# Earlier first transposes, a split up product and moved value copies in a macaron attention block

## The chip, the cores and the metric

The kernel runs on one core of a Trainium2 chip. The metric is the device time of one execution in microseconds (us). Of the kernel before there are three timed runs: 263.29, 265.15 and 265.61, median 265.15 us. One more execution was profiled.

## What is computed

One block of the "macaron" form on x of 2048 rows by 128 features, all in float32. `ffn` is a feed-forward network whose inner part is two butterfly transforms of nine stages; attention is over 16 heads of 8 features and is sparse: a query sees every fourth key, and all keys up to 8 positions away.

```
x = x + 0.5 * ffn(layernorm(x))
x = x + attn(layernorm(x))
x = x + 0.5 * ffn(layernorm(x))

ffn(x):   h = x @ W_exp + b_exp                       # 128 -> 512
          h = gelu(butterfly(h, up_weights) + up_bias)
          y = butterfly(h, down_weights) @ W_con + b_con + down_bias

attn(x):  q, k, v = x @ q_w, x @ k_w, x @ v_w ; q *= sigmoid(unity_scale)
          allowed = (j % 4 == 0) | (abs(i - j) <= 8)
          softmax(where(allowed, q @ k.T / sqrt(8), -inf)) @ v @ o_w + o_b
```

## The kernel before, in words

**Shape of the work.** The 2048 rows are four blocks (`NB`) of 512, each of four tiles (`TB`) of 128 rows. Since nothing non-linear stands inside a butterfly, each is folded with its dense matrix into one 128x512 (`UPW`) or 512x128 (`DNW`) weight while the kernel starts. The order of each engine is written out by hand, an engine runs its own list in order, and semaphores join the lists. PSUM, the memory TensorE writes, has eight banks of 512 columns, `PS[:, 0..7]`.

**The prologue.** TensorE spreads the far stages' weights over all partitions (`spread`), runs a filler product (`keep_warm(1, 1)`, whose output nobody reads), multiplies the folded stages with W_exp (`upw_ps`), transposes the first normalized block (`transpose_block(0)`), makes the bias (`bup_ps`), runs two more fillers (`keep_warm(6, 2)`) and then the first up product (`ffn_up(0)`). VectorE does the stages of folding. ScalarE first takes the sigmoid's exponential of one number that a DMA brings (`ld_un`), then loads the Gelu table, normalizes the first block, copies the spread weights (`SEVENS`), makes eight scaled copies of W_con (`CON8`) and only then copies the transposed block to `XT` (`operand(0)`).

**The first FFN and the projections.** For each block: up product, Gelu on ScalarE, down product (`ffn_down`), sum and layernorm on VectorE, transposes (`turn_rows`), and keys, queries and values (`keys_queries`, `block_values`). VectorE splits keys and queries into three bf16 parts, and SyncE writes the parts to DRAM and loads them back in the layout of attention: the strided keys by `write_strided` and `load_strided`, the local ones by `write_local` and `load_k`. TensorE may start on the strided scores of block c of the keys only when `ld_ks[c]` has come. A test decides whether the softmax needs its maxima: `bound_product` on VectorE makes a number per partition, `count_kept` on TensorE counts them, `bound_flag` on VectorE sets the flag. In the fourth down product the count stands at its half.

**Attention.** 4 blocks by 4 groups of heads give 16 units of nine steps: eight steps of strided scores (two heads by one block of keys, 128x1024 results) and one of local scores. ScalarE takes the exponential of each, VectorE masks the local one (`mask_local`), TensorE forms the value products (`values`, `values_local`), and VectorE and TensorE turn and scale the result (`turn`, `finish_unit`). The last block's own values are computed inside unit 0, after its third step: `block_values(NB - 1)` writes one strided tile and five local ones to banks 6 and 7, and ScalarE's `values_out(NB - 1)` copies them to `VS` and `VL`. Units write their results alternately in banks 6 and 7, so unit 1 may use bank 7 only when it has been copied out.

**The second FFN.** After the last unit: `values(3)`, `values_local`, which waits for VectorE's mask, `transpose_block(NB)`, `turn`, `ffn_up(NB)`, `ctx_turn` and `project`, then three more blocks.

## Time and profile before

| quantity | value |
|---|---|
| median of three runs (lowest to highest) | 265.15 us (263.29 to 265.61) |
| the profiled execution, whole | 265.68 us |
| its span in the trace | 263.7 us |
| TensorE busy | 248.0 us, 94% |
| ScalarE busy | 191.1 us, 72% |
| VectorE busy | 125.4 us, 48% |
| share of TensorE in the chain that ended last | 90% |
| an exponential of 128x1024 on ScalarE | 1.02 us |
| a table load on ScalarE | 1.28 us |
| a whole down product of 32 matmul records | 3.74 us |
| end of VectorE's last split of keys and queries | at 80.3 us |
| start of the fourth step of unit 1 on TensorE | at 84.6 us |

The profile shows when each engine worked on what, by line of the kernel; idle time is given with the event that ended it. A float32 product is recorded as two matmuls and two weight loads, so "x8" is four products. Weight loads of TensorE (PEld) run beside its matmuls (PE). SPq and ACTq are the DMA instructions that SyncE and ScalarE issue.

### The profile page before, as it was taken

Reading aid. Unit: us, or ns where it says so; the run is one execution under the profiler, and the core shown is the slowest. Engines: PE = TensorE matmul, PEld = TensorE weight load, DVE = VectorE, ACT = ScalarE, POOL = GpSimd, SP = SyncE. Lnnn points to the kernel's source line nnn. Section 1 sums busy time; section 2 is a strip of 40 time slices with the busy share of each in tenths; the row PEclk is TensorE's granted clock in tenths of the full one; section 3 lists DMA queues with packets and bytes.
Section 4 is the critical chain, followed back from the end, with each engine's and each line's share of the span. In section 5 each row is a group of like instructions: output and inputs, shape, how many; then the busy total and the mean of one; then the engine's idle time right before and its main releaser. Section 6 shows DMA issues by size and latency. Waiting matters only on the chain.

```text
span 263.7 us, 6909 instructions
## 1 busy us (share of the span) xinstructions
PE 248.0 (94%) x2914; PEld 138.3 (52%) x2914; DVE 125.4 (48%) x408; ACT 191.1 (72%) x245; POOL 7.4 (3%) x12
## 2 busy tenths in 40 slices
PE   0998899998889999999999999999999999899995
PEld 0466585857444444445434455444454444457775
DVE  3689949687793133226234225314325521546013
ACT  1735337383789999988999988999978999653440
POOL 0910000000000000000000000000000000000000
PEclk9999999999999999999999999999999999999999
DMA  5840000386689660330331231232030000000112
GB/s 162 238 137 14 2 0 0 114 240 175 162 208 358 220 144 27 85 88 2 87 86 25 65 87 27 62 87 71 18 87 2 0 2 4 2 0 0 42 40 80
DMA packets 23894, 21.42 MB, mean 81 GB/s; under 512 B 4619, under 2 KB 22095, under 8 KB 23843
## 3 DMA queue, kind: packets, MB, share of 16 engines
q1 hardware_dynamic: 23270, 20.88, 29.2%
q8 instruction: 23, 0.38, 0.6%
q10 hardware_dynamic: 592, 0.09, 0.2%
q14 instruction: 9, 0.07, 0.1%
HBM read 13.60 MB, written 7.56 MB: 80 GB/s over the span
## 4 chain that ended last, share of the span: by engine, by line
PE 90%; ACT 3%; DVE 2%; DMA 2%; issue 1%; ACTq 0%
PE ps L699 23%; PE ps L677 23%; PE ps L517 10%; PE ps L465 9%; PE ps L684 4%; PE ps L709 4%; PE ps L470 2%; PE ps L717 2%; DMA prologue_or_parts<-far_sel 2%; PE ps L553 2%; PE ps L729 1%; PE ps L474 1%; PE ps L448 1%; ACT v_local L841 1%; PE ps L540 1%
## 5 line engine op out<-in xcount | busy, mean ns | idle before, releaser
L902 ACT ACTIVATE probs_all<-ps 128x1024 f32<-128x1024 f32 x128 | 122.8, 1023 | 10.1 <-PE ps L677 9.7
L699 PE MATMUL ps<-probs_all,v_strided 128*32 128x256 f32 x1024 | 68.2, 384 | 1.2 <-ACT v_local L841 1.2
L677 PE MATMUL ps<-q_slots,k_strided 75*128 75x512 bf16 x256 | 66.7, 381 | 0.2 <-ACT probs_all L825 0.2
L699 PEld LDWEIGHTS ps<-probs_all,v_strided 128*32 128x32 f32 x1024 | 27.2, 109 | 32.8 <-issue 9.5
L677 PEld LDWEIGHTS ps<-q_slots,k_strided 75*128 75x128 bf16 x256 | 20.9, 97 | 34.0 <-ACT probs_all L902 9.5
L1210 DVE RECIPROCAL rden<-ps 128x16 f32<-128x16 f32 x16 | 4.1, 258 | 72.1 <-PE ps L717 72.1
L465 PE MATMUL ps<-xnorm_t,up_folded 128*128 128x512 f32 x64 | 29.2, 599 | 1.0 <-ACT xnorm_t L790 1.0
L799 ACT ACTIVATE gelu_h<-ps,bias_up 128x512 f32<-128x512 f32 x24 | 16.1, 687 | 13.0 <-PE ps L465 13.0
L517 PE MATMUL ps<-down_folded,gelu_h 128*128 128x128 f32 x192 | 23.1, 278 | 0.9 <-ACT down_folded L866 0.7
L517 PEld LDWEIGHTS ps<-down_folded,gelu_h 128*128 128x128 f32 x192 | 22.0, 192 | 2.0 <-ACT down_folded L866 0.9
L1236 DVE SCALAR_TENSOR_TENSOR probs_all<-probs_all,mask_k_sb 128x1024 f32<-128x1024 f32 x16 | 19.6, 1224 | 4.0 <-ACT probs_all L908 3.5
L908 ACT ACTIVATE probs_all<-ps 128x1024 f32<-128x1024 f32 x16 | 16.4, 1023 | 3.7 <-PE ps L684 2.1
L465 PEld LDWEIGHTS ps<-xnorm_t,up_folded 128*128 128x128 f32 x64 | 11.7, 192 | 14.0 <-issue 11.9
L1075 DVE SCALAR_TENSOR_TENSOR resid<-ps,resid 128x512 f32<-128x512 f32 (+1 forms) x10 | 5.8, 584 | 22.3 <-PE ps L517 22.3
L1207 DVE COPY o_sb<-ps 128x256 f32<-128x256 f32 x16 | 6.8, 425 | 12.4 <-PE ps L709 12.2
L684 PEld LDWEIGHTS ps<-q_slots,k_local 75*64 75x64 bf16 x512 | 9.3, 112 | 5.9 <-ACT probs_all L902 5.3
L969 DVE TENSOR_SCALAR xnorm<-resid,mean_var,rstd 128x128 f32<-128x128 f32 x44 | 12.1, 342 | 0.2
L709 PEld LDWEIGHTS ps<-probs_all,v_local 128*32 128x32 f32 x512 | 7.9, 109 | 7.8 <-issue 4.7
L935 DVE BATCH_NORM_STATS2 stats<-resid 128x6 f32<-128x128 f32 x48 | 10.3, 280 | 3.1 <-DMA resid<-L_attn_x 2.9
L709 PE MATMUL ps<-probs_all,v_local 128*32 128x64 f32 x512 | 10.5, 222 | 1.0 <-DVE probs_all L1236 1.0
L684 PE MATMUL ps<-q_slots,k_local 75*64 75x64 bf16 x512 | 11.1, 197 | 0.0
L799 ACT ACTIVATE probs_all<-ps,bias_up 128x512 f32<-128x512 f32 x8 | 5.5, 687 | 6.5 <-PE ps L465 6.5
(137 smaller groups left out, 219.2 us busy)
## 6 DMA issues: line engine op xcount, KB each, us to landing
q_slots<-q_parts SPq DMA_DIRECT2D x16, 288.0 KB
k_local<-k_local_parts SPq DMA_DIRECT2D x48, 78.0 KB
q_parts<-prologue_or_parts SPq DMA_DIRECT2D x9, 384.0 KB, 4.4
k_strided<-k_strided_parts SPq DMA_DIRECT2D x12, 96.0 KB
q_parts<-last_parts SPq DMA_DIRECT2D x3, 384.0 KB, 4.9
k_local_parts<-prologue_or_parts SPq DMA_DIRECT2D x3, 288.0 KB, 5.0
resid<-L_attn_x SPq DMA_DIRECT2D x1, 768.0 KB, 8.5
out<-resid SPq DMA_DIRECT2D x3, 256.0 KB, 2.3
```

The lines of the kernel that those rows point to most:

```text
L465: pe.matmul(PS[:, 1 + c, :], UPW[:, c * P:(c + 1) * P], XT[:, :], start=True, stop=True).then_inc(h_ps, 1)
L517: mm = pe.matmul(down_bank(b, t)[:, t * P:(t + 1) * P], hidden(b)[:, c, t * P:(t + 1) * P], DNW[:, c, :], start=(c == 0), stop=(c == NC - 1))
L677: mm = pe.matmul(PS[:, b0 + i, :], KS[:, ch, G * g + h, :], QS[:, g, h, :], start=True, stop=True)
L684: mm = pe.matmul(PS[r * W:(r + 1) * W, b0 + h // 2, (h % 2 * TB + t) * W:(h % 2 * TB + t + 1) * W], KL[:, g, h, w * WSTEP:w * WSTEP + W], ...
L699: mm = pe.matmul(PS[VC * h:VC * (h + 1), 6 + n % 2, 0:QB // 2], VS[:, ch, at:at + VC], probs, start=(ch == 0 and r == 0), stop=False, skip ...
L709: mm = pe.matmul(PS[VC * h:VC * (h + 1), 6 + n % 2, t * W:(t + 1) * W], VL[:, TB * it + t, at:at + VC], PL[:, h, t, :], start=False, stop= ...
L799: act.activation(hidden(b)[:, c, :], PS[:, 1 + c, :], ACT.Gelu, bias=BUP[:, c:c + 1]).then_inc(g_ready, 1)
L902: act.activation(PE_[:, ch // 2, 2 * m:2 * m + 2, ch % 2, :], PS[:, b0:b0 + 2, :], ACT.Exp).then_inc(p_ready, 1)
L908: act.activation(PL[:, :, :, :].rearrange("p h t q -> p (h t q)"), PS[:, b0:b0 + 2, :].rearrange("p a b -> p (a b)"), ACT.Exp).then_inc(p_ ...
L935: ln_link(dve.bn_stats(STAT[:, t, :], X[:, t, :]))
L969: dve.tensor_scalar(xn[:, t, :], X[:, i, :], MV[:, i, 0:1], RS[:, i:i + 1], ALU.subtract, ALU.mult).then_inc(done, 1)
L1236: dve.scalar_tensor_tensor(pl, pl, 3.0e38, band, ALU.min, ALU.mult).then_inc(pl_ready, 1)
```

## The change

The second FFN's first transposes come ahead of the last local value products, and half of its first up product ahead of the last turn. In the prologue the first filler is gone and the first block's transposes take its place; on ScalarE the copy of the transposed block moves ahead of the scaled copies, and the sigmoid and the Gelu table behind it. In the fourth down product the count moves from its half to its last quarter, and on VectorE the bias addition moves behind the three small operations that feed the count. Of the last block's local values four tiles now go to bank 7 alone and are copied by VectorE (`last_values`), behind its last splits; ScalarE copies the strided tile and one local tile. Unit 1 waits for `vl_last` before it first writes bank 7.

```diff
--- before.py
+++ after.py
@@ -206,6 +206,7 @@
         qkv_ps = sem("qkv_ps")
         qk_ready = sem("qk_ready")
         v_ready = sem("v_ready")
+        vl_last = sem("vl_last")
         split = sem("split")
         ks_out = [sem(f"ks_out{b}") for b in range(NB)]
         kl_out = [sem(f"kl_out{b}") for b in range(NB)]
@@ -480,14 +481,13 @@
             spread(0, 1).then_inc(six_bc, 1)
             for r in range(1, NC):
                 spread(r, 1).then_inc(wbc, 1)
+            pe.wait_ge(ld_id, 16)
+            transpose_block(0)
             pe.wait_ge(ld_wt, 16)
-            keep_warm(1, 1)
             pe.wait_ge(up_fold, STAGES - 3)
             for c in range(NC):
                 mm = pe.matmul(PS[:, 1, c * P:(c + 1) * P], WT[:, c, :], UPB[STAGES - 3][:, c * P:(c + 1) * P], start=True, stop=True)
             mm.then_inc(upw_ps, 1)
-            pe.wait_ge(ld_id, 16)
-            transpose_block(0)
             pe.wait_ge(ld_bx, 16 * 2)
             for j in range(NC):
                 mm = pe.matmul(PS[:, 3, j:j + 1], UPB[STAGES - 3][:, j * P:(j + 1) * P], BEX[:, j:j + 1], start=True, stop=True)
@@ -510,9 +510,9 @@
                     pe.wait_ge(y_done, b)
                 for t in range(TB):
                     if last and t == 2:
-                        if b < NB:
-                            count_kept()
                         pe.wait_ge(y_done, b)
+                    if b == NB - 1 and t == TB - 1:
+                        count_kept()
                     for c in range(NC):
                         mm = pe.matmul(down_bank(b, t)[:, t * P:(t + 1) * P], hidden(b)[:, c, t * P:(t + 1) * P], DNW[:, c, :],
                                        start=(c == 0), stop=(c == NC - 1))
@@ -549,8 +549,9 @@
                     pe.wait_ge(qtr_ready, b + 1)
                     mm = pe.matmul(PS[:, bank, 0:P], XTS[:, b, :], VW[:, :], start=True, stop=True)
                 for n, t in list(enumerate(pairs_of(b), 1))[first:end]:
+                    at = n + 2 if b == NB - 1 and n > 1 else n
                     for r in range(2):
-                        mm = pe.matmul(PS[r * W:(r + 1) * W, bank + n // TB, n % TB * P:(n % TB + 1) * P],
+                        mm = pe.matmul(PS[r * W:(r + 1) * W, bank + at // TB, at % TB * P:(at % TB + 1) * P],
                                        XTL[:, (2 * t + r) * WSTEP:(2 * t + r) * WSTEP + W], VW[:, :], start=True, stop=True)
                 if end is None:
                     mm.then_inc(qkv_ps, 1)
@@ -744,6 +745,8 @@
                             block_values(NB - 1, 0, None)
                         if it == 0 and g == 0 and s == 3:
                             pe.wait_ge(v_ready, 3 * NB)
+                        if it == 0 and g == 1 and s == 3:
+                            pe.wait_ge(vl_last, 2)
                         if before and s == 1:
                             values(*before, 3)
                         if before and s == 3:
@@ -757,10 +760,11 @@
                         if s == 0 and it and g == 1:
                             project(it - 1)
             values(NB - 1, NG - 1, 3)
+            transpose_block(NB)
             values_local(NB - 1, NG - 1)
-            transpose_block(NB)
+            ffn_up(NB, range(2))
             turn(NB - 1, NG - 1)
-            ffn_up(NB)
+            ffn_up(NB, range(2, NC))
             ctx_turn(NB - 1)
 
             transpose_block(NB + 1)
@@ -833,7 +837,7 @@
             def values_out(b):
                 act.wait_ge(qkv_ps, 4 * b + 4)
                 vps = (PS[:, 3:5, :] if b < NB - 1 else PS[:, 6:8, :]).rearrange("p a b -> p (a b)")
-                n = len(pairs_of(b))
+                n = len(pairs_of(b)) if b < NB - 1 else 1
                 act.activation(VS[:, b, 0:NH * VSW].rearrange("p (h k) -> p h k", h=NH)[:, :, V1:V1 + D],
                                vps[:, 0:P].rearrange("p (h d) -> p h d", d=D), ACT.Copy).then_inc(v_ready, 1)
                 for r in range(2):
@@ -841,15 +845,16 @@
                     act.activation(VL[rows, ts, 0:NH * VLW].rearrange("p t (h k) -> p t h k", h=NH)[:, :, :, r * V1:r * V1 + D],
                                    vps[rows, P:(n + 1) * P].rearrange("p (t h d) -> p t h d", t=n, d=D), ACT.Copy).then_inc(v_ready, 1)
 
-            act.wait_ge(ld_un, 16)
-            act.activation(SG[:, 0:1], UN[:, :], ACT.Exp, scale=-1.0).then_inc(sig, 1)
-            act.wait_ge(sig, 1)
-            act.activation(SG[:, 3:4], SG[:, 0:1], ACT.Gelu).then_inc(table, 1)
             act.wait_ge(xb_ready, 1)
             for t in range(TB):
                 act.activation(XN[:, 0, t, :], X[:, t, :], ACT.Identity, bias=XB[:, t:t + 1], scale=RS[:, t:t + 1]).then_inc(xn_ready, 1)
             act.wait_ge(wbc, 3)
             act.activation(SEVENS, PS[:, 6:8, :].rearrange("p a b -> p (a b)"), ACT.Copy).then_inc(sev_sb, 1)
+            operand(0)
+            act.wait_ge(ld_un, 16)
+            act.activation(SG[:, 0:1], UN[:, :], ACT.Exp, scale=-1.0).then_inc(sig, 1)
+            act.wait_ge(sig, 1)
+            act.activation(SG[:, 3:4], SG[:, 0:1], ACT.Gelu).then_inc(table, 1)
             act.wait_ge(ld_dn, 16)
             act.wait_ge(ld_wc, 16)
             for h in range(2):
@@ -857,7 +862,6 @@
                     n = h * NC + m
                     ins = act.activation(CON8[:, n * P:(n + 1) * P], WCON[:, 2 * h + m // 2, :], ACT.Copy, scale=WDN[:, n:n + 1])
             ins.then_inc(wc_far, 1)
-            operand(0)
             for b in range(NB + 1):
                 if b < NB:
                     gelu(b)
@@ -1076,11 +1080,11 @@
                                          ALU.mult, ALU.add).then_inc(done, 1)
 
             def ffn_sum(b):
-                add_bias(b)
-                dve.wait_ge(r_ready, b + 2)
                 last = b % NB == NB - 1
                 if last and b < NB:
                     bound_product()
+                add_bias(b)
+                dve.wait_ge(r_ready, b + 2)
                 if last:
                     dve.wait_ge(y_half, b // NB + 1)
                     sum_tiles(b, 0, 2, y_first)
@@ -1199,6 +1203,20 @@
 
 
             dve.wait_ge(qx_ready, TB * NB)
+
+            def last_values():
+
+                dve.wait_ge(qkv_ps, 4 * NB)
+                dve.wait_ge(v_ones, 3)
+                pairs = pairs_of(NB - 1)[1:]
+                n = len(pairs)
+                for r in range(2):
+                    rows, ts = slice(r * W, (r + 1) * W), slice(pairs[0], pairs[0] + n)
+                    dve.tensor_copy(VL[rows, ts, 0:NH * VLW].rearrange("p t (h k) -> p t h k", h=NH)[:, :, :, r * V1:r * V1 + D],
+                                    PS[rows, 7, 0:n * P].rearrange("p (t h d) -> p t h d", t=n, d=D)).then_inc(vl_last, 1)
+
+            last_values()
+
             def finish_unit(it, g):
                 n = NG * it + g
                 dve.wait_ge(o_ps, n + 1)
```

What changes on the engines, at three places. The first is TensorE's list from the spread of the weights (the first row) to the first up product (`ps<-xnorm_t,up_folded`); `ident_sb,xnorm` are the transposes, and the rows `ps<-prologue_or_parts 128x512` behind the first are fillers. Before:

```order
L474 MATMUL ps<-prologue_or_parts 128x512 x8
L470 MATMUL ps<-prologue_or_parts 128x512
L487 MATMUL ps<-probs_all,prologue_or_parts 128x128 x4
L448 MATMUL ps<-ident_sb,xnorm 128x128 x4
L493 MATMUL ps<-b_exp_sb,probs_all 128x1 x4
L470 MATMUL ps<-prologue_or_parts 128x512 x2
L465 MATMUL ps<-xnorm_t,up_folded 128x512 x4
```

And now:

```order
L475 MATMUL ps<-prologue_or_parts 128x512 x8
L449 MATMUL ps<-ident_sb,xnorm 128x128 x4
L489 MATMUL ps<-probs_all,prologue_or_parts 128x128 x4
L493 MATMUL ps<-b_exp_sb,probs_all 128x1 x4
L471 MATMUL ps<-prologue_or_parts 128x512 x2
L466 MATMUL ps<-xnorm_t,up_folded 128x512 x4
```

One filler is gone and the transposes stand before the folding products. The second place is ScalarE's list in the same stretch, from its first table load to the first Gelu (`gelu_h`); `xnorm_t` is the copy of the transposed block. Before:

```order
L845 ACT_TABLE_LOAD
L845 ACTIVATE sigm<-unity_sb 128x1
L847 ACT_TABLE_LOAD
L847 ACTIVATE sigm<-sigm 128x1
L850 ACTIVATE xnorm<-resid,minus_mean_rstd,rstd 128x128 x4
L852 ACTIVATE probs_all<-ps 128x1024
L858 ACTIVATE probs_all<-w_con_sb,prologue_or_parts 128x128 x8
L790 ACTIVATE xnorm_t<-ps 128x512
L799 ACTIVATE gelu_h<-ps,bias_up 128x512 x4
```

And now:

```order
L850 ACT_TABLE_LOAD
L850 ACTIVATE xnorm<-resid,minus_mean_rstd,rstd 128x128 x4
L852 ACTIVATE probs_all<-ps 128x1024
L794 ACTIVATE xnorm_t<-ps 128x512
L855 ACTIVATE sigm<-unity_sb 128x1
L857 ACT_TABLE_LOAD
L857 ACTIVATE sigm<-sigm 128x1
L863 ACTIVATE probs_all<-w_con_sb,prologue_or_parts 128x128 x8
L803 ACTIVATE gelu_h<-ps,bias_up 128x512 x4
```

The normalization no longer stands behind the one number of the sigmoid, and there are still two table loads. The third place is TensorE's list at the end of the last unit, from the last strided value products to the copy of the context; `v_local` are the local value products, `ident_sb,o_sb` is the turn, `ident_sb,ctx_rows` the context's transposes. Before:

```order
L699 MATMUL ps<-probs_all,v_strided 32x256 x8
L709 MATMUL ps<-probs_all,v_local 32x64 x16
L448 MATMUL ps<-ident_sb,xnorm 128x128 x4
L717 MATMUL ps<-ident_sb,o_sb 128x128 x2
L465 MATMUL ps<-xnorm_t,up_folded 128x512 x4
L723 MATMUL ps<-ident_sb,ctx_rows 128x128 x4
```

And now:

```order
L700 MATMUL ps<-probs_all,v_strided 32x256 x8
L449 MATMUL ps<-ident_sb,xnorm 128x128 x4
L710 MATMUL ps<-probs_all,v_local 32x64 x16
L466 MATMUL ps<-xnorm_t,up_folded 128x512 x2
L718 MATMUL ps<-ident_sb,o_sb 128x128 x2
L466 MATMUL ps<-xnorm_t,up_folded 128x512 x2
L724 MATMUL ps<-ident_sb,ctx_rows 128x128 x4
```

The transposes stand before the local value products, and the up product is in two halves around the turn.

## Rows read from the trace of the kernel before

**Rows 1.** The chain that ended last, prologue: start us, us, what.
```profile
9.93 2.01 PE ps L470 x2
11.94 1.71 PE ps L487 x8
13.64 0.85 PE ps L448 x4
...
15.99 3.26 PE ps L470 x4
19.26 3.43 PE ps L465 x8
```
**Rows 2.** Timeline, prologue (start us, us, what, idle before); one row of `ident_sb`.
```profile
6.84 0.16 DVE L994 SCALAR_TENSOR_TENSOR minus_mean_rstd<-mean_var,rstd 128x4 f32<-128x4 f32 x1
...
8.27 0.20 ACT L845 ACTIVATE sigm<-unity_sb 128x1 f32<-128x1 f32 x1 [2.51 <-DMA unity_sb<-L_attn_unity_scale]
...
10.02 0.69 DVE L982 TENSOR_TENSOR probs_all<-probs_all,ps 128x512 f32<-128x512 f32 x1 [1.58 <-PE ps L474]
...
12.34 2.44 ACT L858 ACTIVATE probs_all<-w_con_sb,prologue_or_parts 128x128 f32<-128x128 f32 x8
...
13.68 1.23 DVE L982 TENSOR_TENSOR probs_all<-ps,probs_all 128x1024 f32<-128x1024 f32 x1 [0.89 <-PE ps L487]
...
18.00 0.16 DVE L1043 TENSOR_TENSOR bias_up<-bias_up,up_bias_sb 128x4 f32<-128x4 f32 x1
...
2.94 0.44 ACTq L782 DMA_DIRECT2D ident_sb<-ident  x1
...
DMA to landing us min/median/max: 5.6/5.6/5.6
```
**Rows 3.** Busy time by stretch: stretch, its length, engines, granted clock, DMA share, GB/s.
```profile
18.00:19.00 1.00, 1.00 (x2) 0.34 (x2) 0.96 (x3) 0.00 (x0) 0.00 (x0) 1.00 0.00 0
```
**Rows 4.** Timeline around the fourth down product, TensorE and VectorE, and the chain's bias addition.
```profile
59.13 2.05 PE L517 MATMUL ps<-down_folded,gelu_h 128*128 128x128 f32 x16 [0.22 <-ACT gelu_h L799]
62.25 0.19 PE L586 MATMUL ps<-minus_one,bound_kept 128*1 128x1 f32 x2 [1.07 <-DVE bound_kept L1126]
...
60.84 0.70 DVE resid L976
...
61.95 0.15 DVE L1126 TENSOR_SCALAR bound_kept<-bound_product 128x1 f32<-128x1 f32 x1
```
**Rows 5.** Timeline in unit 0: ScalarE's value copies, TensorE behind them.
```profile
75.28 0.28 ACT L837 ACTIVATE v_strided<-ps 128x128 f32<-128x128 f32 x1 [0.40 <-PE ps L553]
75.45 1.51 ACT L841 ACTIVATE v_local<-ps 64x640 f32<-64x640 f32 x2
...
77.01 1.07 PE L699 MATMUL ps<-probs_all,v_strided 128*32 128x256 f32 x16 [1.24 <-ACT v_local L841]
...
78.01 0.11 PEld L677 LDWEIGHTS ps<-q_slots,k_strided 75*128 75x128 bf16 x2 [0.41 <-DMA k_strided<-k_strided_parts]
```
**Rows 6.** Timeline of SyncE's DMA issues around the third block's strided keys.
```profile
66.22 2.40 SPq L337 DMA_DIRECT2D k_local<-k_local_parts  x6
69.82 0.38 SPq L311 DMA_DIRECT2D k_strided_parts<-prologue_or_parts  x1
...
73.65 2.59 SPq L316 DMA_DIRECT2D k_strided<-k_strided_parts  x6
```
**Rows 7.** Timeline at the end of attention and the start of the second FFN.
```profile
227.47 0.66 PE L709 MATMUL ps<-probs_all,v_local 128*32 128x64 f32 x32 [1.01 <-DVE probs_all L1236]
...
228.67 0.44 PE L717 MATMUL ps<-ident_sb,o_sb 128*128 128x128 f32 x2
228.75 0.60 ACT L790 ACTIVATE xnorm_t<-ps 128x512 f32<-128x512 f32 x1 [1.08 <-PE ps L448]
...
229.40 3.70 PE L465 MATMUL ps<-xnorm_t,up_folded 128*128 128x512 f32 x8 [0.29 <-ACT xnorm_t L790]
...
233.57 0.69 DVE L1223 COPY ctx_t<-ps 128x512 f32<-128x512 f32 x1 [2.16 <-PE ps L723]
```

## The prediction

> **What bounds the kernel now.** Three views were read. The page first: it gives the span, 263.7 us, with TensorE busy for 94% of it (the table above); around it the profiled execution has 265.68 - 263.7 = 2.0 us that no engine works in. Its time stands 0.5 above the median of the runs, 265.15, and the lowest of the three is 2.4 below it. Then the chain of waits in order of time: nearly every piece of it is TensorE's, back to back, so a microsecond is won only where TensorE either works on something that could be left out or stands idle. Last the timelines around each such place. There are four, and the change touches all of them: the prologue, where a product that only keeps the array busy stands between the far-stage products and the first real one [rows 1]; the fourth down product, which stands idle at its half for a count that VectorE has not made ready [rows 4]; the first attention unit, which waits for ScalarE's copies of the last block's values [rows 5]; and the end of attention, where TensorE idles during the last mask and again for the first copy of the second FFN's input [rows 7].
>
> **1, the prologue.** Before, TensorE runs from 9.93: one filler product 2.01, four folding products 1.71, four transposes 0.85, then, between 14.49 and 15.99, four bias products of 1.50 in all, two filler products 3.26, and the first up product at 19.26 [rows 1]. The first filler is taken out and the transposes move into its place. Are they ready at 9.93? Their identity was issued at 2.94 and landed 5.6 later, at 8.5 [rows 2]. The normalized block was late only because ScalarE waited for the one number of the sigmoid until 8.27 [rows 2] and then loaded a table; with that behind it, the four normalizations (they lie between the sigmoid and the transposes; four 128x128 of ScalarE are half of the 2.44 of eight [rows 2], so 1.2 to 1.7) can start when VectorE has the last scalar of the moments, 6.84 + 0.16 = 7.0 [rows 2], and end at about 8.7. So the transposes run 9.93 to 10.78. The folding products need VectorE's piece that ends at 10.02 + 0.69 = 10.71 [rows 2], so they start at about 10.95 and end at 12.65; bias products to 14.15; fillers to about 17.5. That is 1.75 earlier than 19.26. The other gates: VectorE's next step began at 13.68 after an idle 0.89 that the folding products ended [rows 2]. They end 1.0 earlier, so VectorE gains its whole idle 0.89. The last that the up product needs of it, the bias, ends at 18.00 + 0.16 - 0.89 = 17.3 [rows 2], before 17.5, under the fillers; the folded weights come before it. ScalarE's eight scaled copies (2.44) now come behind the sigmoid and the Gelu table: from 11.0 (its 128x1024 copy waits for 9.93 and takes 1.0, as each 128x1024 does in the table), the copy of the transposes 0.6, one table load of 1.28 (the table) and two single elements about 1.6, then 2.44, done at about 15.7. VectorE wants them at about 17.2, so that costs nothing; the cover is 1.5 us.
>
> What the 1.75 is worth hangs on the clock. The granted clock reads 1.00 in the stretch 18 to 19 [rows 3], and in every stretch I asked for, so it can't be read there; the durations can. Two 512-column fillers take 3.26, or 1.63 each, and the four up products after them 3.43, or 0.86 each [rows 1]: the first is the 1.2 GHz level, the second 2.4, and the change falls at about 19, after TensorE had been busy without a gap since 9.93 at least. If it comes that much earlier too, all of 1.75 is kept. If it comes at 19 as before, the up products run at half rate from 17.5 to 19, do 0.75 of their 3.43 in those 1.5, and end at 21.7 instead of 22.7: 1.0 is kept. I take the middle, **1.4**. The Trainium skill (TensorE: Matmul & The Clock Gate, Part 1, the HAM clock gate) says that the slow level is the default, that activity releases it, and that the point varies from run to run with the same kernel. By that the removed filler was activity, its removal speaks against the change, and the value would be nearer 1.0; the even busyness of the rest agrees with either, since no run here shows the prologue without it.
>
> **2, the fourth down product.** TensorE starts it at 59.13, is through its first half after 2.05, and issues the count at 62.25 after an idle 1.07; VectorE made the count's operand at 61.95 to 62.1, behind a bias addition of 0.70 [rows 4]. Now the product's third quarter (0.86 of issue) stands ahead of the count and the bias addition behind the three small operations, which then end at about 61.5. Neither waits. The two halves join without a drain: 32 matmuls take 3.74 in a whole down product (the table), so the end is 59.13 + 3.74 + 0.2 for the count = 63.1; before, it was 62.25 + 0.1 + 2.05 = 64.4. The sum and the layernorm behind it on VectorE start as much earlier, down to the 0.1 by which its flag ends later. I take **1.2** (bounds: 1.07, the idle alone, and 1.3).
>
> **3, the last values.** Before, ScalarE copies the strided values (0.28) and two lots of five local tiles (1.51) from 75.28 on, and TensorE's first value products wait until 77.01 [rows 5]. Now ScalarE copies one tile twice. A 128-wide copy takes 0.28 with 0.17 from start to start [rows 5], so it ends at about 75.9 and the value products start 1.05 earlier. VectorE copies the other four tiles in two copies of 64x512 (at most 0.69 each, as a 128x512 copy from the same memory in [rows 7]) behind its last split, from 80.3 to 81.7; TensorE asks for them ahead of the fourth step of unit 1, at 84.6 before (both times in the table), and both move with the rest, so no cost.
>
> But the next scores want the third block's strided keys. Their weight load at 78.01 was ended by that DMA, in an idle stretch of 0.41 that began at 77.60 [rows 5]; so the keys landed between 77.60 and 78.0. What is saved ahead of them is therefore given back unless the DMA moves too. Part 3 does not move it: of its 1.05, only **0.2** (0 to 0.4) is left. Part 2 moves it if the queue does: SyncE issued the keys' write at 69.82, right behind VectorE's split, which follows the down product, and had been free since 66.22 + 2.40 = 68.62; the loads went out at 73.65 [rows 6]. So the write can go out 1.2 earlier, by exactly the gap. It took 3.8 to land, with twelve loads of local keys issued around it. I let 1.0 of the 1.2 through. Part 2 and 3 together: 1.0 + 0.2 = **1.2**, with both ends 0.2 and 2.25. The Trainium skill (DMA: Bandwidth & Descriptors, Queues, rings and completion order) says that each DMA engine consumes one queue's descriptors in ring order. By that, the write only joins the local keys' loads sooner, and lands where it did: 0.2 instead of 1.2.
>
> **4, the end.** The four transposes (0.60 after the local products) fit into the idle 1.01 ahead of 227.47. ScalarE's input copy began at 228.75 after an idle 1.08, so it can begin at 227.67 and end at 228.27; the local products end at 228.1, and the up product starts at 228.3 instead of 229.40 [rows 7], 1.1 earlier. Two of its four products, 1.72, now come ahead of the turn, which moves from 228.67 to 230.0. The turn's 0.2 now lies inside the up product rather than in idle time, so TensorE is through 0.9 earlier. VectorE, which needs the turn for its last context rows, idled 2.16 before the context copy at 233.57 [rows 7]; it starts 1.3 later and is wanted 0.9 earlier, which that 2.16 just covers. Later up and down products have no waits in the chain. I take **0.9** (bounds 0.6, if VectorE's order costs some tenths, and 1.1).
>
> **Sum**: 1.4 + 1.2 + 0.9 = 3.5. From the profiled execution's 265.68 that is 262.2, from the median 261.7; I say 262.0. About 1%, 2.65 us, is what a measurement of this kernel can tell from no change.
>
> **Rivals.** *Both soft terms give way*: the clock rises at 19 as before and the keys land where they did: 1.0 + 0.2 + 0.9 = 2.1, or 263.3, no difference that can be told. For it speaks that the write took 3.8 from issue; against it that the loads behind that write took 4.0 to 4.4 themselves, from 73.65 to between 77.6 and 78.0, with fewer transfers around them, so most of either time goes with its issue. *Both come out whole*: 1.75 + 2.25 + 1.0 = 5.0, or 260.4: the write's long landing would have to shrink by 1 us. *Slower*: without the filler TensorE stays at the half rate past the first FFN block. The gain ahead of it is 1.75 + 1.2 + 0.9 = 3.85; each microsecond of real work at the half rate loses half of one. It is used up if the half rate lasts 7.7 us beyond 17.5, to 25, and the time is 1% above if it lasts to 30.5, or 267.8. What speaks for it is that TensorE was slow for 9 us of unbroken work, from 9.93 to 19, already; against it, that it has no gap now either, and that its work from the bias products on is the same as before. The Trainium skill's rule of a default slow level, named above, is this rival's. *The order doesn't matter*: if the second FFN's early half only exchanges idle places, part 4 gives 0.3 and the whole 2.9: it is in the first case's range.
>
> **Numbers.** Forecast (261.2 to 263.0 by the bounds of its terms) 0.60, a fifth of it short of 1%; soft terms give way 0.22; both whole 0.14; slower 0.04. Faster by over 1%: 0.48 + 0.14 + a part of the second case whose before is the higher median, 0.03 = 0.65; slower by over 1% 0.03; within 1% the other 0.32. The range of 260.6 to 264.2 leaves out most of the slow tail and the far end of the whole gain, and holds the 2.3 us by which runs of one kernel differ only in part.
>
> **What would show it.** Right: no filler at 9.9 and the first up product near 17.5; no idle ahead of the count; the first value products within 0.7 us of the start of ScalarE's value copies; a wait of about 0.9 on the strided keys' DMA just behind them; the up product within 1 us of the end of the last mask. Wrong: up products of 1.7 each past 22 (clock), a keys' wait of 2 (queue), or VectorE ahead of the context copy.

## The result and the profile after

The changed kernel takes 261.83 us (median of 20 runs, 260.23 to 269.09) against 264.11 of the kernel before (20 runs beside them): ratio 0.9892, 95% interval 0.9869 to 0.9915, so about 2.85 us or 1.1% less (the medians stand 2.28 apart; the ratio leaves disturbed runs out and is what counts). Three runs stood behind the 265.15 shown above; the median of twenty is 1.0 lower. The profiled execution after took 262.01 us, 3.67 less than that of before.

| | before | after |
|---|---|---|
| median us | 264.11 | 261.83 |
| profiled execution, its span | 265.68, 263.7 | 262.01, 260.2 |
| first up product starts | 19.26 | 17.54 |
| first up product ends | 22.69 | 21.64 |
| idle before the count | 1.07 | none |
| first value products start, behind the start of ScalarE's copies | 1.73 | 0.81 |
| second FFN's first up product, behind the end of the last mask | 1.98 | 0.79 |

The page of the kernel after: the span, TensorE's busy time, and the chain's shares by engine.

```profile
span 260.2 us, 6909 instructions
...
PE 247.2 (95%) x2912; PEld 137.8 (53%) x2912; DVE 126.7 (49%) x410; ACT 190.5 (73%) x245; POOL 7.4 (3%) x12
...
PE 85%; DMA 6%; DVE 3%; ACT 2%; SPq 2%; issue 1%; ACTq 0%
```

TensorE is the bound as before. Now the four places. First the chain of waits of after in the prologue (start us, us, what), to be read against [rows 1]:

```profile
5.64 3.80 PE ps L475 x16
...
9.46 1.11 PE ps L449 x4
10.57 1.85 PE ps L489 x8
12.41 1.50 PE ps L493 x8
13.91 3.62 PE ps L471 x4
17.54 4.10 PE ps L466 x8
21.64 0.91 PE ps L501 x8
```

The first filler is gone and the up product starts at 17.54. But it takes 4.10 instead of 3.43, so of 1.72 at its start 1.05 is left at its end, and 0.49 of that was there already at the first row: the spread of the weights began at 5.64, not 6.13, since its weight DMA landed sooner. Why the product is longer is seen in the timeline of TensorE's weight loads (start us, us, what, idle before), first of after, then of before:

```profile
17.33 0.34 PEld L466 LDWEIGHTS ps<-xnorm_t,up_folded 128*128 128x128 f32 x1 [0.52 <-issue]
...
18.90 0.19 PEld L466 LDWEIGHTS ps<-xnorm_t,up_folded 128*128 128x128 f32 x1 [0.38 <-issue]
```
```profile
18.56 0.30 PEld L465 LDWEIGHTS ps<-xnorm_t,up_folded 128*128 128x128 f32 x1 [0.52 <-issue]
19.09 0.19 PEld L465 LDWEIGHTS ps<-xnorm_t,up_folded 128*128 128x128 f32 x1 [0.24 <-issue]
```

A 128x128 load takes 0.34 at the 1.2 GHz level and 0.19 at 2.4. The first at 0.19 comes at 18.90, where in before it came at 19.09: the clock rose when it had risen before, though the work stood 1.7 earlier. In before it rose inside the second filler, and in after only inside the up product. The granted clock reads 1.00 through all of it.

The fourth down product of after, TensorE's timeline, against [rows 4]:

```profile
58.07 2.94 PE L517 MATMUL ps<-down_folded,gelu_h 128*128 128x128 f32 x24 [0.22 <-ACT gelu_h L803]
60.95 0.19 PE L587 MATMUL ps<-minus_one,bound_kept 128*1 128x1 f32 x2
61.06 1.16 PE L517 MATMUL ps<-down_folded,gelu_h 128*128 128x128 f32 x8
```

Three quarters, the count, the last quarter, no wait. Then the first attention unit of after, ScalarE's value copies and TensorE behind them, against [rows 5]:

```profile
73.08 0.28 ACT L841 ACTIVATE v_strided<-ps 128x128 f32<-128x128 f32 x1 [0.40 <-PE ps L554]
73.26 0.57 ACT L845 ACTIVATE v_local<-ps 64x128 f32<-64x128 f32 x2
...
73.89 1.07 PE L700 MATMUL ps<-probs_all,v_strided 128*32 128x256 f32 x16 [0.31 <-ACT v_local L845]
...
75.48 1.04 PE L678 MATMUL ps<-q_slots,k_strided 75*128 75x512 bf16 x4 [0.53 <-DMA k_strided<-k_strided_parts]
```

The wait for the copies shrank from 1.24 to 0.31, and the wait for the third block's strided keys just behind grew. Their write and loads are SyncE's issues in the same timeline, against [rows 6]:

```profile
67.72 0.38 SPq L312 DMA_DIRECT2D k_strided_parts<-prologue_or_parts  x1
...
71.54 2.97 SPq L317 DMA_DIRECT2D k_strided<-k_strided_parts  x6
```

Both are 2.1 earlier than before, and 3.82 apart where they were 3.83 apart. Last the end of attention, all engines' timeline of after, against [rows 7]:

```profile
224.94 0.65 PE L710 MATMUL ps<-probs_all,v_local 128*32 128x64 f32 x32 [0.42 <-DVE probs_all L1254]
...
225.68 1.98 PE L466 MATMUL ps<-xnorm_t,up_folded 128*128 128x512 f32 x4
...
229.50 0.69 DVE L1239 TENSOR_TENSOR resid<-resid,o_bias 128x512 f32<-128x512 f32 x1
...
230.11 0.69 DVE L1241 COPY ctx_t<-ps 128x512 f32<-128x512 f32 x1
...
230.85 1.16 PE L730 MATMUL ps<-o_w_sb,ctx_t 128*128 128x128 f32 x8 [0.37 <-DVE ctx_t L1241]
```

The idle before the last local products fell from 1.01 to 0.42, the up product follows them with no idle, and VectorE's idle of 2.16 ahead of the context copy is gone: it comes right behind the bias addition.

To put a number on each place in every kernel, the traces were cut at the same instructions. *Spread* is the start of the first spread product; *up start* and *up end* are those of the first up product, counted from there; *down* runs from the start of the fourth down product to the key product behind it; *values* from that key product to the first value products, *scores* from it to the third pair of scores (the ones that want the third block's keys); *end* from the last local exponential to the start of the last FFN's closing sum. The stretches between these are the same in all traces (36.43 to 36.45 and 147.1 to 147.2).

| kernel | spread | up start | up end | down | values | scores | end |
|---|---|---|---|---|---|---|---|
| before | 6.13 | 13.13 | 16.56 | 5.12 | 12.76 | 13.76 | 35.86 |
| after | 5.64 | 11.90 | 16.00 | 3.99 | 11.83 | 13.42 | 34.91 |
| change_again | 5.46 | 12.02 | 15.82 | 3.99 | 11.83 | 13.48 | 34.91 |
| u_prologue | 5.42 | 11.36 | 15.03 | 3.99 | 11.83 | 13.10 | 34.91 |
| u_prologue_again | 5.66 | 11.12 | 14.79 | 3.99 | 11.82 | 13.19 | 34.91 |
| u_count | 5.64 | 11.89 | 16.06 | 5.12 | 11.83 | 13.36 | 34.91 |
| u_copies | 5.43 | 13.04 | 16.74 | 3.99 | 12.75 | 13.75 | 34.91 |
| u_end | 5.42 | 11.89 | 16.11 | 3.99 | 11.84 | 13.26 | 35.85 |
| f_back | 5.97 | 13.76 | 17.19 | 3.99 | 11.83 | 13.33 | 34.91 |
| f_one | 5.54 | 10.70 | 16.35 | 3.99 | 11.83 | 12.99 | 34.90 |
| f_none | 5.36 | 10.61 | 16.75 | 3.99 | 11.82 | 13.01 | 34.91 |
| d_keys | 5.30 | 11.92 | 15.35 | 3.99 | 11.83 | 13.30 | 34.91 |
| d_keys2 | 5.50 | 10.78 | 14.45 | 3.99 | 11.83 | 12.83 | 34.91 |
| combo | 5.32 | 10.62 | 14.29 | 3.99 | 11.82 | 12.83 | 34.89 |

From before to after: 0.49 by the weight DMA (not the change's: it is anywhere from 5.30 to 6.13 in these kernels), 0.56 in the prologue, 1.13 at the count, 0.34 at the keys, 0.95 at the end, 3.47 of the 3.5 between the spans. The four that are the change's make 2.98, beside 2.85 by the times.

### The profile page after: what moved, and what is told of

Read it like the earlier page. It is cut to its first block, busy times and chain, and to the rows that moved or that the text cites. A ratio compares the mean times of both kernels' runs of the same rounds, so it can differ in the third digit from the quotient of the medians.

```text
span 260.2 us, 6909 instructions
## 1 busy us (share of the span) xinstructions
PE 247.2 (95%) x2912; PEld 137.8 (53%) x2912; DVE 126.7 (49%) x410; ACT 190.5 (73%) x245; POOL 7.4 (3%) x12
## 4 chain that ended last, share of the span: by engine, by line
PE 85%; DMA 6%; DVE 3%; ACT 2%; SPq 2%; issue 1%; ACTq 0%
PE ps L700 23%; PE ps L678 23%; PE ps L517 10%; PE ps L466 9%; PE ps L685 4%; PE ps L710 3%; DMA k_strided_parts<-prologue_or_parts 3%; PE ps L718 2%; PE ps L471 2%; PE ps L730 1%; PE ps L475 1%; DMA prologue_or_parts<-far_sel 1%; PE ps L449 1%; DMA k_strided<-k_strided_parts 1%; SPq L338 1%
## 5 line engine op out<-in xcount | busy, mean ns | idle before, releaser
L906 ACT ACTIVATE probs_all<-ps 128x1024 f32<-128x1024 f32 x128 | 123.0, 1022 | 10.5 <-PE ps L678 10.0
L466 PE MATMUL ps<-xnorm_t,up_folded 128*128 128x512 f32 x64 | 30.1, 611 | 0.8 <-ACT xnorm_t L794 0.7
L803 ACT ACTIVATE gelu_h<-ps,bias_up 128x512 f32<-128x512 f32 x24 | 16.1, 687 | 12.3 <-PE ps L466 12.2
L710 PE MATMUL ps<-probs_all,v_local 128*32 128x64 f32 x512 | 10.5, 222 | 0.4 <-DVE probs_all L1254 0.4
```

The costliest lines, as they stand in the source:

```text
L466: pe.matmul(PS[:, 1 + c, :], UPW[:, c * P:(c + 1) * P], XT[:, :], start=True, stop=True).then_inc(h_ps, 1)
L710: mm = pe.matmul(PS[VC * h:VC * (h + 1), 6 + n % 2, t * W:(t + 1) * W], VL[:, TB * it + t, at:at + VC], PL[:, h, t, :], start=False, stop= ...
L803: act.activation(hidden(b)[:, c, :], PS[:, 1 + c, :], ACT.Gelu, bias=BUP[:, c:c + 1]).then_inc(g_ready, 1)
L906: act.activation(PE_[:, ch // 2, 2 * m:2 * m + 2, ch % 2, :], PS[:, b0:b0 + 2, :], ACT.Exp).then_inc(p_ready, 1)
```

## The experiments: each part undone

Four kernels are the changed kernel with one part undone. The prologue:

```diff
@@ TensorE
-            pe.wait_ge(ld_id, 16)
-            transpose_block(0)
             pe.wait_ge(ld_wt, 16)
+            keep_warm(1, 1)
             pe.wait_ge(up_fold, STAGES - 3)
...
             mm.then_inc(upw_ps, 1)
+            pe.wait_ge(ld_id, 16)
+            transpose_block(0)
@@ ScalarE
-            operand(0)
-            (sigmoid and Gelu table: from here to ahead of the normalizations)
...
             ins.then_inc(wc_far, 1)
+            operand(0)
```

> The change with its prologue undone (filler, transposes and ScalarE's order as before); the other three parts stay. My theory: the prologue is worth 1.0 to 1.7 us depending on when the clock rises, so this one lies about 1.2 us above the change: the up product starts 13.1 us after the first spread product, against 11.9 with the change, and its four products take 3.4 at full rate. Rival: the clock takes it all, and the 1.06 us by which the changed kernel's trace was ahead came from a weight DMA that landed 0.5 us sooner there; then this one is no more than 0.5 us slower than the change.

Measured: 261.25 us, ratio to before 0.9896 (0.985 to 0.9941), no slower than the change with its 0.9892. Its trace has the filler, and the up product at full rate all the same. Chain of waits, then the eight weight loads of the bias products, in this kernel and in before:

```profile
9.22 2.00 PE ps L471 x2
11.22 1.72 PE ps L488 x8
...
16.21 0.44 DVE up_folded L1039
...
16.78 3.67 PE ps L466 x8
```
```profile
13.36 1.27 PEld L494 LDWEIGHTS ps<-b_exp_sb,probs_all 128*128 128x128 f32 x8
```
```profile
14.08 1.83 PEld L493 LDWEIGHTS ps<-b_exp_sb,probs_all 128*128 128x128 f32 x8
```

The eight loads take 1.27 here and 1.83 in before: the clock rose inside them. Taken one by one, the fourth is the first of 0.19, at 13.99, five microseconds ahead of before's 19.09, with the prologue in before's order. So the order does not by itself fix the point, and before's one trace, on which the prediction's 1.4 rests, was a late one. And with an early rise the up product meets another bound: its matmuls stand idle 0.24 behind the last filler for VectorE's folded weights, which end at 16.65. A second run under the same edit, u_prologue_again, is told further down.

The count and the bias addition put back:

```diff
                     if last and t == 2:
+                        if b < NB:
+                            count_kept()
                         pe.wait_ge(y_done, b)
-                    if b == NB - 1 and t == TB - 1:
-                        count_kept()
...
             def ffn_sum(b):
+                add_bias(b)
+                dve.wait_ge(r_ready, b + 2)
                 last = b % NB == NB - 1
                 if last and b < NB:
                     bound_product()
-                add_bias(b)
-                dve.wait_ge(r_ready, b + 2)
```

> The change with the place of the count and of VectorE's bias addition undone. My theory: TensorE idles 1.07 us ahead of the count again, but of that only what the strided keys' DMA followed is lost: the keys' write goes out 1.1 us later and the keys land later by as much, so the wait for them at the second pair of steps in unit 0 stays near 0.5 us and the kernel is 1.1 us slower than the change. Rival: the DMA queue sets the landing of the keys whatever the issue; then the wait for the keys shrinks to nothing, the keys land where they did, and the kernel is at most 0.6 us slower than the change.

Measured: 263.33 us, 0.9948 (0.9913 to 0.9983), 1.5 us slower than the change. Timeline, TensorE and SyncE:

```profile
61.26 0.19 PE L587 MATMUL ps<-minus_one,bound_kept 128*1 128x1 f32 x2 [1.06 <-DVE bound_kept L1130]
...
76.62 1.04 PE L678 MATMUL ps<-q_slots,k_strided 75*128 75x512 bf16 x4 [0.45 <-DMA k_strided<-k_strided_parts]
...
68.84 0.38 SPq L312 DMA_DIRECT2D k_strided_parts<-prologue_or_parts  x1
...
72.26 3.21 SPq L317 DMA_DIRECT2D k_strided<-k_strided_parts  x6
```

The idle of 1.06 is back and *down* is 5.12 again, 1.13 more. The write of the keys goes out 1.12 later than in after, and *scores* stays 13.36 against 13.42: the keys land as much later as the work does. Had the write only joined a queue whose content fixes the landing, the keys would have landed where they do in after, and the wait of 0.45 would be gone. That rival falls.

ScalarE copies all the last values:

```diff
-                    at = n + 2 if b == NB - 1 and n > 1 else n
+                    at = n
...
-                n = len(pairs_of(b)) if b < NB - 1 else 1
+                n = len(pairs_of(b))
...
-            last_values()
```

> The change with the copies of the last block's local values undone (ScalarE makes all of them). My theory: the value products start 0.9 us later, but the next step waits for the strided keys in the changed kernel until 75.5 anyway, so only 0.3 us is lost (0.2 to 0.5), and the wait for the keys' DMA is gone from TensorE's matmuls. Rival: the copies' part is worth its whole 0.9 us, and the keys came late in the changed kernel's trace by chance.

Measured: 262.49 us, 0.9921 (0.9888 to 0.9955). Timeline of TensorE in the first unit:

```profile
75.36 1.07 PE L700 MATMUL ps<-probs_all,v_strided 128*32 128x256 f32 x16 [1.24 <-ACT v_local L843]
76.36 1.04 PE L678 MATMUL ps<-q_slots,k_strided 75*128 75x512 bf16 x4
```

The wait for the copies is before's 1.24, and behind it the keys are not waited for any more. *Values* is 0.92 later than in after, *scores* only 0.33. So the copies are worth 0.3, and what lies between is the keys' wait. The same trace shows in the chain that the transposes can wait for their identity:

```profile
2.94 7.54 DMA ident_sb<-ident
...
10.52 1.12 PE ps L449 x4
```

It landed at 10.48, two microseconds after the 8.5 of [rows 2], and put this kernel's up product 1.1 later. With that trace's prologue late for a reason that is not the edit's, its time alone does not price the copies; the stretches do.

The order at the end put back:

```diff
-            transpose_block(NB)
             values_local(NB - 1, NG - 1)
-            ffn_up(NB, range(2))
+            transpose_block(NB)
             turn(NB - 1, NG - 1)
-            ffn_up(NB, range(2, NC))
+            ffn_up(NB)
```

> The change with the end of attention undone. My theory: 0.95 us slower than the change: the first up product starts 2.9 us after the end of the last strided value products instead of 2.8 less 1.2, and the context copy waits for TensorE again instead of following VectorE's bias addition without idle time. Rival: the early half of the up product is given back whole by the later turn, since VectorE's normalization and bias addition stand between the turn and the context copy: then it is within 0.3 us of the change.

Measured: 263.06 us, 0.9958 (0.993 to 0.9985), 1.7 slower than the change; *end* is 35.85, 0.94 more, with all else as in after. Chain of waits:

```profile
226.59 3.70 PE ps L466 x8
230.29 0.45 PE ps L724 x4
...
230.77 0.70 DVE ctx_t L1240
```

By the times the four parts are worth 0.1, 1.5, 0.8 and 1.7 us, each good to about 1; by the traces 0.56, 1.13, 0.34 and 0.95. The count and the end are told from nothing by both, the copies by the traces alone.

## The experiments: fillers and the clock

Three kernels change the fillers of the changed kernel. f_back has the removed one again, behind the transposes; f_one halves the two that stay ahead of the up product; f_none takes them out.

```diff
@@ f_back
             pe.wait_ge(ld_wt, 16)
+            keep_warm(1, 1)
             pe.wait_ge(up_fold, STAGES - 3)
@@ f_one
-            keep_warm(6, 2)
+            keep_warm(6, 1)
@@ f_none
-            keep_warm(6, 2)
```

> The changed kernel with the removed filler product put back between the transposes and the folding products. It tells whether the removed filler cost time or held the clock up. My theory before this run: the filler is 0.9 to 1.7 us of path and the clock rises at about 18.7 us of the span in most runs anyway, so this one is 0.5 to 1 us slower than the change. Rival (the runs so far allow it, since in the kernel with the old prologue the weight loads went to 0.19 us as early as 14.9): the filler's work makes the early rise likelier, and in such runs the up product starts by VectorE's folded weights at about 16.1; then it is equal to the change or up to 1 us faster, and most of its runs lie in the lower of the two groups of times.

> The changed kernel with one filler instead of two ahead of the first up product. If the real up product does for the clock what the filler does, the up product starts at 16.5 instead of 17.5, runs at half rate until about 18.7 and ends at 21.1 instead of 21.6: 0.5 us faster than the change. Rival: the clock rises later for the missing filler, and the kernel is equal or slower.

> The changed kernel without any filler ahead of the first up product: TensorE then idles from about 14 until VectorE's folded weights are there at 16.1. If the clock only asks for work, not for unbroken work, the up product starts at 16.2 and ends near 21. If the idle 2 us put the rise off, the up product and the folding of the down weights run at half rate beyond 20 us of the span and the kernel is 1 to 3 us slower than the change: the mechanism of the rival that ended on the slower side.

Measured: f_back 262.37 us, 0.9932 (0.9901 to 0.9963); f_one 262.37, 0.9951 (0.9917 to 0.9985); f_none 262.83, 0.9954 (0.9927 to 0.9981). Their chains: f_back's filler and up product, then f_one's up product and f_none's; and last f_none's first weight load of 0.19.

```profile
11.21 1.71 PE ps L471 x2
...
19.73 3.43 PE ps L466 x8
```
```profile
16.24 5.65 PE ps L466 x8
```
```profile
15.97 6.14 PE ps L466 x8
```
```profile
21.10 0.19 PEld L466 LDWEIGHTS ps<-xnorm_t,up_folded 128*128 128x128 f32 x1 [0.39 <-issue]
```

In f_back the filler takes its 1.71 on the path, and the first fast load comes at 19.54: *up end* is 17.19, 1.19 later than in after (about 0.3 of it by an identity that landed at 10.05), and by the ratios the kernel is 1.06 us slower. So taking that filler out was right, and the rise did not need it. With the other two fillers it is the reverse. f_one and f_none start the up product 1.2 to 1.3 earlier after the spread (10.70 and 10.61) and end it 0.35 and 0.75 later: the rise came at 20.44 and 21.10, so the up product ran at the 1.2 GHz level for most of its length, 5.65 and 6.14 against 4.10. TensorE's matmuls stood idle 2.35 before the up product in f_none, waiting for VectorE's folded weights, and only 0.07 in f_one, so the idle time alone does not tell when the clock rises. By the ratios f_one and f_none are both 1.6 us slower than the change, where the first was expected to be 0.5 faster; that is more than *up end* shows, so part of it lies in runs that have no trace. The "slower" rival's mechanism is there, but at 1.6 us, far from the 3.85 that it had to use up.

The first fast load in all fourteen traces, in us of the span and taken load by load: in the old prologue 19.09 (before), 13.99, 12.54; in the new one with its two fillers 18.90, 18.12, 18.96, 19.00, 18.79, 17.06, 12.42, 12.26; with the filler back 19.54; with one 20.44 and none 21.10. Both orders can have it early or late. What decides is not settled by these runs.

## The experiments: the keys, and the parts together

If the wait for the third block's keys eats the copies' gain, an earlier write should give it back. d_keys moves the second write and the strided loads ahead of two groups of local keys on SyncE; d_keys2 leaves only one group ahead of the first write.

```diff
@@ d_keys
             write_strided(2)
-            for g in range(2, NG):
-                load_k(0, g, ld_q[g])
             write_strided(NB - 1)
             load_strided(2)
             load_strided(NB - 1)
+            for g in range(2, NG):
+                load_k(0, g, ld_q[g])
@@ d_keys2
-            for g in range(2):
-                load_k(0, g, ld_q[g])
+            load_k(0, 0, ld_q[0])
             write_strided(2)
-            for g in range(2, NG):
-                load_k(0, g, ld_q[g])
             write_strided(NB - 1)
             load_strided(2)
             load_strided(NB - 1)
+            for g in range(1, NG):
+                load_k(0, g, ld_q[g])
```

> The changed kernel with SyncE's issues reordered: both writes of strided key parts and the loads of strided key blocks 2 and 3 come before the loads of local keys for units 2 and 3. Six of the twelve local loads are then no longer in the queue around them. Theory that the queue makes the keys late: keys of block 2 land 1 us or more earlier, the wait of 0.53 us on TensorE ahead of the third pair of scores is gone, and the kernel is 0.5 us faster than the change. Rival, that the landing is latency behind VectorE's split: the write still lands 3.8 us after its issue, and nothing changes.

> The changed kernel with only the first group's local keys loaded ahead of the write of block 2's strided keys; the other three groups' loads come behind the strided loads. In all traces so far that write took 3.4 to 3.9 us from issue to the start of the loads behind it, whether or not local loads followed it, while the next write, issued 2 to 3 us later, was through in 0.4 to 2.3. If the three local loads issued just ahead of it hold it up, it takes 2.5 us or less now, TensorE's wait for the keys (0.2 to 0.5 us) is gone and 0.4 us is saved. If it is plain latency it stays at 3.4 or more.

Measured: d_keys 261.75 us, 0.9904 (0.9873 to 0.9935); the write took 3.74 to the loads' issue and the wait stayed, 0.40. That the local loads behind the write were what held it falls: taking them away is worth 0.1 at most. d_keys2 260.54 us, 0.9863 (0.9814 to 0.9911). Its timeline, SyncE, then TensorE:

```profile
65.96 0.38 SPq L312 DMA_DIRECT2D k_strided_parts<-prologue_or_parts  x1
...
69.38 2.36 SPq L317 DMA_DIRECT2D k_strided<-k_strided_parts  x6
...
73.22 1.04 PE L677 MATMUL ps<-q_slots,k_strided 75*128 75x512 bf16 x4
```

No wait for the keys, and *scores* is 12.83, the 0.93 of the copies kept whole; combo, below, has the same. The traces hold the time at which the last of the keys landed: 6.9 and 7.1 behind the write's issue in these two kernels, 7.3 to 7.7 in the others with two groups of local loads ahead of the write and ScalarE's copies as in the change. In those *scores* varies from 12.99 to 13.48, so part of the round trip varies by itself, and two traces make the new order's gain likely and no more. From write to the loads' issue it is 3.3 to 3.9 over all kernels, with or without local loads behind it: that is the time of the write itself, whose landing stands right ahead of the loads' issue in every trace. It is 3.42 here, not the 2.5 that was expected if the loads ahead of it held it up.

The last four ran together on one chip: the change once more, the prologue undone once more, d_keys2, and combo, which adds to d_keys2 the identity's DMA ahead of the scalar's on ScalarE, and on VectorE the normalization of the next FFN block behind the bias addition and copy of the last context.

```diff
@@ ScalarE
+            act.dma_start(ID[:, :], ident).then_inc(ld_id, 16)
             act.dma_start(UN[:, :], ...).then_inc(ld_un, 16)
-            act.dma_start(ID[:, :], ident).then_inc(ld_id, 16)
@@ VectorE
             finish_unit(NB - 1, NG - 1)
-            ffn_ahead(NB + 1)
             finish_block(NB - 1)
+            ffn_ahead(NB + 1)
```

> The changed kernel once more, on the chip of the three others of this group, so that they are compared with it there. Expected: 2.6 to 3.0 us under the kernel before, as in its first measurement (ratio 0.989).

> The change with the prologue undone, once more, beside the change itself. My theory after the first runs: the reordered prologue is worth 0.5 to 1 us (the kernel with the filler put back was about 1 us slower), so this one has a ratio 0.002 to 0.004 above the change. Rival: the old order lets the clock rise early in more runs and the new one makes the transposes wait for the identity's DMA (until 9.6 to 10.5 us of the span in four traces), which eats the gain: then the ratio is the same within 0.001 and the prologue's term of the sum was worth nothing.

> The changed kernel with three more edits: SyncE's order as in the kernel of this group with one local load ahead; the identity's DMA issued ahead of the single number's on ScalarE; VectorE's last early normalization behind the second-last block's work, so that the context copy no longer follows it. Expected by stage: the transposes start at the end of the spread products in any run, not at the identity's landing (0 to 1 us, 0.3 on average); the context copy waits for TensorE again (0.25 us); the keys up to 0.4. Together 0.5 to 1 us under the change. Rival: each of these is hidden and the time is that of the change.

Measured: the change 261.56 us, 0.9863 (0.9815 to 0.991); prologue undone 260.97, 0.9874 (0.983 to 0.9918); combo 261.19, 0.9876 (0.9829 to 0.9923). The prologue undone is again no slower, 0.3 us by the ratios and inside their error. combo's trace is the shortest, span 257.5, and that owes most to an early clock: *up end* 14.29, beside d_keys2's 14.45. Its chain at the end:

```profile
226.99 0.45 PE ps L723 x4
...
227.47 0.70 DVE ctx_t L1240
```

The context copy now waits for TensorE's context transposes, and they end, counted from the first up product, where the copy started in after (4.40 against 4.43): *end* is 34.89 against 34.91. The two engines were level there, so moving VectorE alone gives 0.02. combo's 0.5 to 1 us under the change did not come: no version is measurably ahead of the change; d_keys2 has the lowest median, 1.0 under the change's on the same chip, with intervals that overlap.

## Why the prediction was right, and where it was not

The time came at 261.83 against 262.0 said, inside 260.6 to 264.2, and the likeliest case held. That it came within 0.2 is in part luck. The sum was 3.5, and the change's own parts gave 2.98 in the traces and 2.85 by the times; but the median before was really 264.11, a microsecond under the 265.15 that the sum was set against, and the profiled execution's 262.01 had 0.49 of help from the weight DMA. Step by step:

- **Part 1, said 1.4, measured 0.56: mis-sized.** Three steps failed. The first is the path. That the up product started at 17.54 with 17.5 said is luck: the spread stood 0.49 earlier, and counted from there the path shortened 1.23 and not 1.75. The transposes took 1.11 where 0.85 was allowed, and the two fillers 3.62 where 3.26 was; the 3.26 of before is not a time at the 1.2 GHz level throughout, since the clock rose inside the second filler. The second is "I take the middle": the clock rose at 18.9 as before, and the up product took 4.10. The low end was 1.0, and with the shorter path 0.56 is left of it. The third cost little in after: "landed 5.6 later, at 8.5" was one trace's value. In after the identity landed at 9.45, just as the spread ended, and cost at most 0.07 (the transposes take 1.04 where it landed earlier); in five other traces of this order it held the transposes up by 0.2 to 1.3. Compared at an early rise in both, the gain is 0.3 to 0.7 (*up end* 14.79 and 15.03 against 14.45 and 14.29), for then both orders wait for VectorE's folded weights: TensorE's matmuls stand idle 0.24 and 0.80 in the old one, 1.21 and 1.13 in the new. By the times it is 0.1 to 0.3, inside the error. The rule of the Trainium skill (TensorE: Matmul & The Clock Gate, Part 1, the HAM clock gate), that activity releases the slow level and that the point varies from run to run, agrees with the runs: 12.3 to 19.1 with work unbroken from 10.5 on at the latest, later with fewer fillers. The page puts the variation at half a microsecond either way; here it is far larger, and the measurement decides.
- **Part 2, said 1.2 with the keys' DMA following by 1.0: right.** 1.13 on TensorE, and the DMA followed whole (u_count). The ring-order rule of the Trainium skill (DMA: Bandwidth & Descriptors, Queues, rings and completion order) would have given 0.2 here; no run shows it at work on this write, whose loads follow 3.3 to 3.9 after its issue wherever it is put.
- **Part 3, said 0.2 (0 to 0.4): right.** 0.34 in after, 0.3 to 0.8 over the kernels that have it and the change's SyncE order. The mechanism is shown from both sides: with the copies undone the keys' wait is gone, and with the keys earlier the copies' 0.93 is kept. The size is partly luck: in before the keys landed at 77.89, 0.12 ahead of the load that wanted them, and the rest of the 0.34 is a round trip that took 7.7 in after and 8.1 in before.
- **Part 4, said 0.9 (0.6 to 1.1): right.** 0.95 by the trace. The "2.16 which just covers" held to a few hundredths. One sign of being wrong did appear, VectorE's work ahead of the context copy in the chain, and combo shows it to be worth 0.02.
- **The rivals.** "Both soft terms give way" came half: the clock did, the keys didn't. "Slower" did not occur in the change; its mechanism cost 1.6 us in f_one and in f_none, under half of what it needed. "The order doesn't matter" falls with u_end.
- Of what was to show it, the wait on the keys, put at 0.9, was 1.01 on TensorE's weight loads, where the 0.41 of [rows 5] stands, and 0.53 on its matmuls. The value products stood 0.81 behind the copies' start and not 0.7, because ScalarE's two one-tile copies took 0.57 where 0.45 was allowed.

## What to carry to other kernels

A gain ahead of a wait for a transfer is kept only as far as the transfer moves too: look for what issues it, and price the two apart (0.93 was won at the values and 0.34 left at the scores). Work moved ahead of the clock's rise is done at the slow rate, so a microsecond saved there is worth about half (1.23 on the path left 0.56 here), and one trace does not tell when the rise comes; a filler is judged by where the first real product *ends*, not where it starts. A landing time read in one trace is a sample too, when the change takes its slack away.

## What the runs showed of the hardware

- With the same order of work TensorE's first fast weight load came anywhere from 12.3 to 19.0 us of the span in the new prologue, and from 12.5 to 19.1 in the old; times of before lie around 263.3 to 264.6 and 265.1 to 266.0, and of after around 260.2 to 261.0 and 261.8 to 262.8, a distance that fits an early and a late rise (argued from the traces, not shown run by run).
- The granted clock read 1.00 while 512-column products took 1.7 instead of 0.86; the weight load's duration, 0.34 or 0.19, tells the level where that column does not.
- Key parts written to DRAM and read back take 3.3 to 3.9 from the write's issue to the loads', with or without local loads issued between.
- The same identity DMA, issued at 2.94 by the same code, had landed by 8.5 in one trace and landed at 10.5 in another.
